# Experts' up/gate bias: from a product on TensorE to a copy by ScalarE into the PSUM bank

## The chip, the core and the metric

One core of a Trainium2 chip runs the whole program. The metric is device time in microseconds, the median over repeated runs; lower is better.

## What is computed

The reference is a transformer block on x of 2 x 2048 tokens, 256 wide, in float32: attention with a latent of 64 and 16 heads, then two rounds (C = 2) of a mixture of experts with a shared expert. What the change touches is one round's experts:

```python
h = jnp.einsum('nh,ehi->eni', xf, exp_Wup) + exp_bup[:, None, :]
h = jax.nn.silu(jnp.einsum('eni,eij->enj', h, exp_Wg) + exp_bg[:, None, :]) * h
eo = jnp.einsum('eni,eih->enh', h, exp_Wdown) + exp_bdown[:, None, :]
combined = jnp.einsum('ne,enh->nh', weights, eo)
```

Six experts, of which each token takes two. The biases are not zero in the inputs.

## The kernel before

`build` runs the attention first and then `build_mixture`, whose engine programs are in `build_tokens`. Every engine has its program written out by hand; semaphores (`S[...]`) order them. Float32 operands are split in a hi part (rounded for the matrix engine) and a lo part, and a product is three products: hi by hi, hi by lo, lo by hi.

A round goes over 8 blocks of 512 tokens: router, choice of two experts per token (`choose`), shared expert. The tokens of one batch element (a group of 4 blocks) are then scattered by GpSimd to `x_slots` in DRAM, sorted by expert in tiles of 128 rows that belong to one expert each (37 tiles a group). The expert stage `tiles(c)` of round c runs over 2 x 37 tiles: `tiles(0)` and `tiles(1)` are 148 tiles. While a group's tiles run, GpSimd scatters the second group or gathers the first one's results, and VectorE adds gathered rows (`add_first`, `add_second`, at every other tile from a group's sixth on in the second half of the stage) and normalizes a finished block (`normalize`, at three tiles of each stage).

One expert tile t goes through these steps, all in double buffers (t % 2):

- SyncE `load_tile` (L1282): slots to `xg`, four buffers; in the queue's program, load of t+3 stands ahead of the store of t-3, which waits until ScalarE has written that tile's result.
- TensorE `turn_tile` (L1599): reads the tile's expert number into a register (L1596, one load per tile), two transposes. Then `tile_up`: a product that writes the expert's up and gate bias (512 columns) into the bank `TU + t % 2`, made of a one-hot column `pick` and the table `W["bias"]` (L1604, hi and lo rows in one product), and six products of 512 columns onto it (L1615). `turn_gated` (L1628): two transposes. `tile_down`: the down bias (L1604, 256 columns) and six products of 256 columns (L1645).
- ScalarE: `tile_hi` (L1784) hi half of the tile, `tile_silu` (L1790), `tile_ghi` (L1796) hi half of the gated rows, `tile_out` (L1802) result to `eo`, `square` (L1810) for the normalization. In the loop over t they stand in the order silu(t), out(t-2), ghi(t-1), hi(t+2), square.
- VectorE: `tile_gated` (L2318), `tile_glo` (L2322), `tile_lo` (L2311), in the order gated(t), glo(t-1), lo(t+2), then adds and normalizations.

TensorE's order in the loop:

```python
for t in range(first, end + 2):
    if t < end:
        tile_up(t)
    if t == 0:
        shared_down(7)
    if t - 2 >= first:
        tile_down(t - 2)
    if first <= t - 1 < end:
        turn_gated(t - 1)
    if t + 2 < end:
        turn_tile(t + 2)
```

So the tiles t-2, t-1, t and t+2 are in flight at once. `tile_up(t)` waits for the hi and lo halves of the tile and, as its bank is that of t-2, for gated(t-2).

In `tiles(1)` SyncE also reads ahead, for the blocks to be finished, the accumulator (`load_acc`, L1301) and the layer's input x1 (L1303), 512 KB each, at four tiles, and at one tile `load_kept` (L1313, L1314), four transfers of 512 KB.

Of the kernel before, what the change touches and what calls it, by code (L numbers as in the profile page):

```python
# [21 lines left out]
F32 = mybir.dt.float32  # L22
# [1116 lines left out]
def build_tokens(nc, W, F, w, x_v, out_v, y_v, x_slots, e_slots, acc_dram, x1_dram):  # L1139

    with ExitStack() as ctx:
        names = ["small_in", "stage0", "stage1", "filled",
                 "down_in0", "down_in1", "down_in2", "down_in3",
                 "router_hi", "router_lo", "w_hi", "w_lo", "made", "bias_made", "share_bias", "own_bias", "bias_sum", "bias_hi", "bias_lo",
# [9 lines left out]
                 "t_x", "t_hi", "t_lo", "t_up", "t_silu", "t_g", "t_turned", "t_ghi", "t_glo", "t_down", "t_out",  # L1154
# [30 lines left out]
        xt_late = yy[:, :, 0:DT, :]  # L1185

# [4 lines left out]
        def x1_rows(r):  # L1191

            return x1t[:, r % 2] if r < 14 else xcur[:, 0, r % 2]
# [13 lines left out]
        def group_tiles(g):  # L1207
            return range(TILES * g, TILES * (g + 1))

# [13 lines left out]
        with nc.Block() as block:  # L1223
            @block.sync
            def _(sp):
# [45 lines left out]

                def load_tile(t):
# [16 lines left out]
                def load_acc(r):  # L1289
# [12 lines left out]
                    if r >= 8:  # L1302
                        sp.dma_start(x1t[:, r % 2], x1_dram[r - 8]).then_inc(S[f"x1_in{r % 2}"], DMA)  # L1303

                def load_x1(r):
                    sp.wait_ge(S["out_ready"], TPB * (r - 9))
# [38 lines left out]
                for r in blocks(0):  # L1345
# [62 lines left out]
            def _(pe):  # L1408
# [177 lines left out]
                def turn_tile(t):  # L1586
# [9 lines left out]
                    expert[t] = pe.value_load(F["tile_i"][0:1, g % 2, s:s + 1], min_val=0, max_val=E - 1)  # L1596
# [5 lines left out]
                def tile_bias(out, t, cols):  # L1602
                    pick = F["pick"][:, t // TILES % 2, t % TILES:t % TILES + 1].broadcast_to([P, P])
                    return pe.matmul(out, pick, W["bias"][:, cols], start=True, stop=False)  # L1604
# [26 lines left out]
                def tile_down(t):  # L1631
# [10 lines left out]
                    tile_bias(out, t, slice(2 * I, 2 * I + D))  # L1642
# [44 lines left out]
            def _(act):  # L1687
# [63 lines left out]
                def bias_hi():  # L1751
                    act.wait_ge(S["bias_sum"], 4)
                    act.wait_ge(S["filled"], FILLS)
                    act.activation(W["bias"][0:E, :], W["exp_biases"][:, :], ACT.Copy).then_inc(S["bias_hi"], 1)
# [42 lines left out]

                def tile_out(t):
# [757 lines left out]
```

## Time and profile before

| | us |
|---|---|
| median of three runs | 2874.68 |
| lowest, highest | 2870.64, 2879.78 |
| the profiled execution | 2871.32 |
| its span | 2868.5 |

Busy shares of the span: TensorE 93%, its weight loads 77%, VectorE 69%, GpSimd 67%, ScalarE 60%. The attention takes most of the time; of the experts' part, the up products (L1615) are 235.2 us for 888 instructions, the mean of one 401 ns (ends of products are modelled, so neighbours overlap). How to read it: a stage's limit is read from the engine that has no idle time in it, and the distance between the starts of neighbouring products tells what one costs, not its duration.

### The profile page before, as it was taken

The page shows a single profiled execution, that of the slowest core. Times are in us where ns is not written, and L with a number is a line of the kernel's source. Part 1 is how long each engine was busy: PE and PEld are TensorE (multiplying, and loading weights), DVE is VectorE, ACT ScalarE, POOL GpSimd, SP SyncE. Part 2 cuts the span into 40 slices and gives each one's busy share as a digit, 9 for nine tenths or more (in the row PEclk, how much of TensorE's full clock was granted, in tenths as well). Part 3 has the DMA queues.
Part 4 walks back from the last instruction along what each step waited for, and adds up shares of the span by engine and source line. Part 5 has one row for each costly group of instructions (what it writes and reads, how often), then busy time and mean ns, then how long its engine had stood idle before and what let it go on. Part 6 is the DMA issues. An engine that isn't in the chain of part 4 may idle for free. (4 is left out here: it accounts for less than half of the span.)

```text
span 2868.5 us, 47472 instructions
## 1 busy us (share of the span) xinstructions
PE 2681.7 (93%) x13656; PEld 2222.5 (77%) x13656; DVE 1975.1 (69%) x4387; ACT 1724.2 (60%) x4016; POOL 1933.7 (67%) x1735
## 2 busy tenths in 40 slices
PE   7999999999989999999999999799989998879994
PEld 5688888888777888888878888688878887768873
DVE  6688788887887788788887887255744464753455
ACT  2577777777776777777777777633323442224442
POOL 2598998998878888988988989722442232543224
PEclk8799999999999999999999999899999998879997
DMA  3011111111111010111110100154333451224552
GB/s 71 14 40 47 39 40 47 36 33 43 36 42 36 25 27 22 27 33 25 27 33 24 23 23 21 46 178 135 118 125 122 139 151 55 94 98 142 178 164 91
DMA packets 162064, 191.53 MB, mean 67 GB/s; under 512 B 57996, under 2 KB 126866, under 8 KB 161304
## 3 DMA queue, kind: packets, MB, share of 16 engines
q1 hardware_dynamic: 148504, 154.67, 18.6%
q0 software_dynamic: 12288, 33.57, 3.6%
q8 instruction: 122, 2.00, 0.3%
q14 instruction: 126, 1.03, 0.1%
q10 hardware_dynamic: 1024, 0.26, 0.0%
HBM read 114.45 MB, written 83.14 MB: 69 GB/s over the span
## 5 line engine op out<-in xcount | busy, mean ns | idle before, releaser
L305 POOL TENSOR_TENSOR pl<-pr,ph 128x512 fp32r<-128x512 f32 (+3 forms) x1184 | 1373.9, 1184 | 211.2 <-ACT ph L723 189.4
L720 ACT ACTIVATE pr<-ps 128x512 f32<-128x512 f32 (+3 forms) x1280 | 688.0, 538 | 401.6 <-PE ps L473 161.6
L995 DVE TENSOR_REDUCE part<-ps 128x1 f32<-128x512 f32 (+3 forms) x1152 | 704.0, 617 | 137.7 <-PE ps L458 122.5
L723 ACT ACTIVATE ph<-ps 128x512 fp32r<-128x512 f32 (+3 forms) x1280 | 686.7, 537 | 0.0
L458 PE MATMUL ps<-k_hi,q_parts 128*128 128x512 f32 (+3 forms) x1280 | 493.2, 386 | 41.5 <-DVE part L995 36.1
L472 PE MATMUL ps<-q_parts,k_hi 128*128 128x512 f32 (+3 forms) x1280 | 482.5, 377 | 0.3
L473 PE MATMUL ps<-q_row,k_lo 65*128 65x512 f32 (+3 forms) x1280 | 471.3, 368 | 0.0
L458 PEld LDWEIGHTS ps<-k_hi,q_parts 128*128 128x128 f32 x1280 | 243.8, 191 | 137.1 <-DVE part L995 57.9
L472 PEld LDWEIGHTS ps<-q_parts,k_hi 128*128 128x128 f32 x1280 | 242.1, 189 | 55.5 <-ACT ph L723 7.6
L473 PEld LDWEIGHTS ps<-q_row,k_lo 65*128 65x128 f32 x1280 | 242.7, 190 | 34.1
L1895 POOL DMA_INDIRECT x_slots<-xcur,slot_i x128 | 126.1, 985 | 167.7 <-PE ps L1615 80.4
L493 PE MATMUL ps<-ph,nn 128*128 128x512 f32 (+3 forms) x640 | 236.4, 369 | 1.1 <-POOL pl L305 1.1
L493 PE MATMUL ps<-ph,v_hi 128*128 128x512 f32 (+3 forms) x640 | 235.6, 368 | 1.1 <-POOL pl L305 0.9
L1615 PE MATMUL ps<-exp_up,yy 128*128 x888 | 235.2, 401 | 0.0
L494 PE MATMUL ps<-ph,nn 128*128 128x512 f32 (+3 forms) x640 | 234.3, 366 | 0.0
L495 PE MATMUL ps<-pl,nn 128*128 128x512 f32 (+3 forms) x640 | 234.1, 366 | 0.0
L494 PE MATMUL ps<-ph,v_lo 128*128 128x512 f32 (+3 forms) x640 | 233.3, 365 | 0.0
L495 PE MATMUL ps<-pl,v_hi 128*128 128x512 f32 (+3 forms) x640 | 233.3, 364 | 0.0
L904 DVE TENSOR_TENSOR ps<-ps,mask_kq 128x128 f32<-128x128 f32 x512 | 149.9, 293 | 114.2 <-PE ps L473 108.3
L1490 PE MATMUL ps<-xt,share_up 128*128 128x512 f32 x720 | 206.2, 447 | 20.1 <-issue 13.4
L815 POOL TENSOR_TENSOR q_parts<-q_raw,q_parts 64x512 fp32r<-64x512 f32 x128 | 171.2, 1338 | 51.7 <-DVE q_parts L898 41.9
L1907 POOL DMA_INDIRECT yg<-e_slots,slot_i x96 | 92.5, 964 | 163.5 <-PE ps L1615 82.2
(251 smaller groups left out, 4680.1 us busy)
## 6 DMA issues: line engine op xcount, KB each, us to landing
work<-x_slots SPq DMA_DIRECT2D x148, 128.0 KB
e_slots<-work SPq DMA_DIRECT2D x148, 128.0 KB
rec<-recip_rows SPq DMA_DIRECT2D x128, 128.0 KB
y_latent<-y_sums SPq DMA_DIRECT2D x128, 128.0 KB
yg<-y_latent SPq DMA_DIRECT2D x32, 512.0 KB
x_slots<-zero_rows SPq DMA_DIRECT2D x32, 296.0 KB
acc_shared<-accw SPq DMA_DIRECT2D x14, 512.0 KB
accr<-acc_shared SPq DMA_DIRECT2D x12, 512.0 KB, 3.7
```

The lines of the kernel that those rows point to most:

```text
L305: eng.tensor_tensor(pl[:, s % RING, 0:w], pr[:, s % PR_RING, 0:w], f32(ph[:, s % RING, 0:w]), ALU.subtract).then_inc(sem, 1)
L458: pe.matmul(ps[:, MAX_BANK + m % 2, 0:w], qa[half][:, i * P:(i + 1) * P], khs[seq][:, c * BLK:c * BLK + w], start=True, stop=True).then_in ...
L472: pe.matmul(out, khs[p // PAIRS][:, k], qa[half][:, q], start=True, stop=False)
L473: pe.matmul(out, kls[p // PAIRS][0:LD + 1, k], qc[half][:, q], start=False, stop=True).then_inc(S["scored"], 1)
L493: pe.matmul(out, v_hi[:, kt, :], ph[:, b, 0:w], start=kt == 0, stop=False)
L494: pe.matmul(out, v_lo[:, kt, :], ph[:, b, 0:w], start=False, stop=False)
L495: pe.matmul(out, v_hi[:, kt, :], pl[:, b, 0:w], start=False, stop=kt == TPB * (qb + 1) - 1).then_inc(S["latent_used"], 1)
L720: act.activation(pr[:, s % PR_RING, 0:w], src, ACT.Exp).then_inc(S["probs"], 1)
L723: act.activation(ph[:, s % RING, 0:w], src, ACT.Exp).then_inc(S["probs_hi"], 1)
L995: ins = dve.tensor_reduce(dst, src[:, 0:w], AX.X, ALU.max)
L1490: mm = pe.matmul(out, sup[:, a, kind, n, dt, m * P:(m + 1) * P], x_t[:, x, dt, :], start=i == 0, stop=i == len(terms) - 1)
L1615: mm = pe.matmul(out, tx[:, t % 2, x, dt, :], wu[:, b, bass.ds(expert[t], 1), dt, :], start=False, stop=n == len(terms) - 1)
```

## The change

- `tile_bias` is called for the down part alone, and `W["bias"]` shrinks from 768 to 256 columns. The six up products no longer start with a product that clears the bank; all of them add.
- ScalarE's new `tile_seed(t)` copies the expert's 512 bias values, the same in every partition, from a table in SBUF (`x1_table`, six experts) into the tile's bank, at an address made from the expert's number in a register. `tile_up(t)` waits for it instead of for gated(t-2); the seed waits for gated(t-2).
- The table comes from DRAM: SyncE stores the biases when they are complete (block 4) and reads them back broadcast to 128 partitions, 1.5 MB, in block 7, when layer input buffers of the first round, whose memory the table takes, are done.
- ScalarE's order in the loop becomes silu(t), ghi(t-1), hi(t+2), seed(t+2), out(t-2), square.
- The expert numbers are loaded eight at a time (five at a group's end) by TensorE and by ScalarE, without the bounds check that stood behind each load.
- x1 of the blocks 8 to 11 is read into the shared expert's buffer `gg` instead of `x1t`; so the hi part of the gated rows of block 14 waits until these blocks are out. Three small work arrays of VectorE share memory.

```diff
+        def load_experts(engine, t):
+            g, s = t // TILES, t % TILES
+            count = min(EXPERTS_AT_ONCE, TILES - s)
+            _, values = nc.values_load_multi_w_load_instructions(
+                F["tile_i"][0:1, g % 2, s:s + count], engines=[engine], min_val=0, max_val=E - 1,
+                skip_runtime_bounds_check_because="a tile's expert is a sum of five comparisons, so it is 0 to 5")
+            return {t + n: v for n, v in enumerate(values)}
...
+                def keep_biases():
+                    sp.wait_ge(S["bias_sum"], 4)
+                    sp.dma_start(bias_dram, W["exp_biases"][:, :]).then_inc(S["bias_kept"], DMA)
+
+                def load_up_table():
+                    sp.wait_ge(S["bias_kept"], DMA)
+                    sp.wait_ge(S["x_norm"], TPB * 8)
+                    for k in range(2):
+                        sp.wait_ge(S[f"x1_stored{k}"], DMA * 4)
+                    sp.dma_start(up_table, bias_dram[:, 0:2 * I].unsqueeze(0).broadcast_to([P, E, 2 * I])).then_inc(S["up_table_in"], DMA)
...
                     if r >= 8:
-                        sp.dma_start(x1t[:, r % 2], x1_dram[r - 8]).then_inc(S[f"x1_in{r % 2}"], DMA)
+                        sp.dma_start(x1g[:, r % 2], x1_dram[r - 8]).then_inc(S[f"x1_in{r % 2}"], DMA)
 
                 def load_x1(r):
-                    sp.wait_ge(S["out_ready"], TPB * (r - 9))
+                    sp.wait_ge(S["t_seed"], 4 * TILES)
...
+                    if r == 4:
+                        keep_biases()
+                    if r == 7:
+                        load_up_table()
...
-                    expert[t] = pe.value_load(F["tile_i"][0:1, g % 2, s:s + 1], min_val=0, max_val=E - 1)
+                    if s % EXPERTS_AT_ONCE == 0:
+                        expert.update(load_experts(mybir.EngineType.PE, t))
...
                 def tile_up(t):
                     pe.wait_ge(S["t_hi"], t + 1)
                     pe.wait_ge(S["t_lo"], t + 1)
-                    if t % (2 * TILES) >= 2:
-                        pe.wait_ge(S["t_g"], t - 1)
+                    pe.wait_ge(S["t_seed"], t + 1)
                     out = ps[:, TU + t % 2, :]
-                    tile_bias(out, t, slice(0, 2 * I))
...
-                                       start=False, stop=n == len(terms) - 1)
+                                       start=False, stop=n == len(terms) - 1, skip_group_check=True)
...
+                        if r == LATE[0]:
+                            act.wait_ge(S["out_ready"], 4 * TPB)
                         act.activation(gg[:, 0, m, :], g0[:, m, :], ACT.Copy).then_inc(S["g_hi"], 1)
...
+                def tile_seed(t):
+                    g, s = t // TILES, t % TILES
+                    if s == 0:
+                        act.wait_ge(S["tiles"], g + 1)
+                    if t == 0:
+                        act.wait_ge(S["up_table_in"], DMA)
+                    if s % EXPERTS_AT_ONCE == 0:
+                        seeds.update(load_experts(mybir.EngineType.Activation, t))
+                    if t % (2 * TILES) < 2:
+                        act.wait_ge(S["gated"], 4 * (LATE[0] if t >= 2 * TILES else 8))
+                    else:
+                        act.wait_ge(S["t_g"], t - 1)
+                    act.activation(ps[:, TU + t % 2, :], up_table[:, bass.ds(seeds.pop(t), 1), :].rearrange("p a n -> p (a n)"),
+                                   ACT.Copy).then_inc(S["t_seed"], 1)
...
+                    tile_seed(first)
                     tile_hi(first)
+                    tile_seed(first + 1)
                     tile_hi(first + 1)
                     for t in range(first, end + 2):
                         if t < end:
                             tile_silu(t)
-                        if t - 2 >= first:
-                            tile_out(t - 2)
                         if first <= t - 1 < end:
                             tile_ghi(t - 1)
                         if t + 2 < end:
                             tile_hi(t + 2)
+                            tile_seed(t + 2)
+                        if t - 2 >= first:
+                            tile_out(t - 2)
```

## Rows read from the trace of the kernel before

**Rows 1.** The page's first part: busy us (share of the span) and instructions per engine.

```profile
PE 2681.7 (93%) x13656; PEld 2222.5 (77%) x13656; DVE 1975.1 (69%) x4387; ACT 1724.2 (60%) x4016; POOL 1933.7 (67%) x1735
```

**Rows 2.** Busy us by stretch: length, PE, PEld, DVE, ACT, POOL, PEclk, DMA share, GB/s.

```profile
2150.00:2408.00 258.00, 246.46 (x1444) 214.24 (x1444) 124.39 (x324) 110.04 (x341) 68.47 (x70) 0.96 0.40 125
2555.00:2792.00 237.00, 225.66 (x1352) 196.04 (x1352) 119.46 (x320) 105.04 (x333) 66.22 (x69) 0.98 0.47 150
```

**Rows 3.** Timeline of one tile, TensorE: start us, us, engine line op, idle before.

```profile
2328.40 0.28 PE L1604 MATMUL ps<-bias,pick 128*128 128x256 f32 x1
...
2329.23 0.38 PE L1628 MATMUL ps<-ident,work 128*128 128x128 f32 x2
...
2329.59 0.48 PE L1604 MATMUL ps<-bias,pick 128*128 128x512 f32 x1
...
2329.91 1.56 PE L1615 MATMUL ps<-exp_up,yy 128*128 x6
...
2331.07 0.19 PEld L1604 LDWEIGHTS ps<-bias,pick 128*128 128x128 f32 x1
2331.30 0.28 PE L1604 MATMUL ps<-bias,pick 128*128 128x256 f32 x1
```

**Rows 4.** The same timeline, ScalarE, VectorE and SyncE's queue.

```profile
2328.60 0.39 ACT L1790 ACTIVATE work<-ps 128x256 f32<-128x256 f32 x1 [1.13 <-PE ps L1615]
...
2329.43 0.38 ACT L1802 ACTIVATE work<-ps 128x256 f32<-128x256 f32 x1 [0.45 <-PE ps L1645]
...
2329.72 0.38 ACT L1796 ACTIVATE nn<-ps 128x256 fp32r<-128x256 f32 x1
2329.84 0.32 SPq L1287 DMA_DIRECT2D e_slots<-work  x1
...
2329.98 0.39 ACT L1784 ACTIVATE yy<-ps 128x256 fp32r<-128x256 f32 x1
2330.13 0.42 DVE L2322 TENSOR_TENSOR nn<-ps,nn 128x256 fp32r<-128x256 f32 x1 [0.68 <-ACT nn L1796]
2330.21 0.43 SPq L1282 DMA_DIRECT2D work<-x_slots  x1
2330.47 0.41 DVE L2311 TENSOR_TENSOR yy<-ps,yy 128x256 fp32r<-128x256 f32 x1
...
2332.25 0.36 ACT L1790 ACTIVATE work<-ps 128x256 f32<-128x256 f32 x1
...
2332.64 0.43 DVE L2318 TENSOR_TENSOR work<-ps,work 128x256 f32<-128x256 f32 x1 [0.85 <-PE ps L1628]
```

**Rows 5.** Groups by line and shape, ScalarE: busy us, mean ns, idle before.

```profile
L1749 ACT ACTIVATE nn<-yg 128x512 fp32r<-128x512 f32 x6 | 3.5, 623 | 2.8 <-DMA yg<-in_exp_down 2.8
```

**Rows 6.** Line 1596, TensorE's sequencer, whole span: ns min/median/max, first and last start.

```profile
L1596 PEldq TENSOR_LOAD <-tile_i x148: 295/301/762, 2150.8 to 2777.2; - x148
L1596 PEldq FUSED_REGOPS  x148: 151/151/165, 2151.4 to 2777.5; - x148
L1596 PEldq SEQ_ASSERT  x148: 18/18/28, 2151.6 to 2777.7; - x148
```

**Rows 7.** One number load (line's view, short window), and its tile's transposes (timeline).

```profile
L1596 PEldq TENSOR_LOAD <-tile_i x1: 297/297/297, 2270.2 to 2270.2; - x1
...
2271.09 0.25 PEld L1599 LDWEIGHTS ps<-ident,work 128*128 128x128 f32 x2
```

**Rows 8.** Timeline at a tile with two scatters: ScalarE's copy-out, TensorE's weight loads.

```profile
2194.09 0.38 ACT L1802 ACTIVATE work<-ps 128x256 f32<-128x256 f32 x1 [1.32 <-PE ps L1645]
...
2195.28 0.19 PEld L1604 LDWEIGHTS ps<-bias,pick 128*128 128x128 f32 x1 [0.47 <-ACT nn L1796]
2196.65 0.20 PEld L1599 LDWEIGHTS ps<-ident,work 128*128 128x128 f32 x2 [0.18 <-issue]
```

**Rows 9.** Timeline, TensorE's weight loads at two of the six normalization tiles.

```profile
2322.27 0.19 PEld L1604 LDWEIGHTS ps<-bias,pick 128*128 128x128 f32 x1 [0.20 <-issue]
...
2724.29 0.18 PEld L1604 LDWEIGHTS ps<-bias,pick 128*128 128x128 f32 x1 [1.54 <-issue]
```

**Rows 10.** Timeline, second stretch: a late tile load and the transposes that wait for it.

```profile
2699.30 0.82 SPq L1282 DMA_DIRECT2D work<-x_slots  x1
...
2707.99 0.20 PEld L1599 LDWEIGHTS ps<-ident,work 128*128 128x128 f32 x2 [2.79 <-DMA work<-x_slots]
```

More of the change, by code:

```diff
@@ L1136, with build_tokens @@
 LATE = (14, 15)
-def build_tokens(nc, W, F, w, x_v, out_v, y_v, x_slots, e_slots, acc_dram, x1_dram):
+def build_tokens(nc, W, F, w, x_v, out_v, y_v, x_slots, e_slots, acc_dram, x1_dram, bias_dram):
     with ExitStack() as ctx:
@@ L1185, in build_tokens @@
         xt_late = yy[:, :, 0:DT, :]
+        up_table = F["x1_table"][:, :, :]
+        x1g = f32(gg[:, :, :, :]).rearrange("p a m n -> p (a m n)").rearrange("p (k j d) -> p k j d", k=2, d=D)
         def acc_rows(r):
@@ L1191, in x1_rows @@
         def x1_rows(r):
-            return x1t[:, r % 2] if r < 14 else xcur[:, 0, r % 2]
+            return x1g[:, r % 2] if r < 12 else x1t[:, r % 2] if r < 14 else xcur[:, 0, r % 2]
         T_BANK, DOWN_BANK, COUNT_BANK = 6, 4, 2
@@ L1600, in turn_tile, with tile_bias @@
                     mm.then_inc(S["t_x"], 1)
-                def tile_bias(out, t, cols):
+                def tile_bias(out, t):
                     pick = F["pick"][:, t // TILES % 2, t % TILES:t % TILES + 1].broadcast_to([P, P])
-                    return pe.matmul(out, pick, W["bias"][:, cols], start=True, stop=False)
+                    return pe.matmul(out, pick, W["bias"][:, :], start=True, stop=False)
                 def tile_up(t):
@@ L1641, in tile_down @@
                     out = ps[:, TD + t % 2, 0:D]
-                    tile_bias(out, t, slice(2 * I, 2 * I + D))
+                    tile_bias(out, t)
                     terms = [(x, b, it) for x, b in ((0, down_hi), (0, down_lo), (1, down_hi)) for it in range(2)]
@@ L1753, in bias_hi @@
                     act.wait_ge(S["filled"], FILLS)
-                    act.activation(W["bias"][0:E, :], W["exp_biases"][:, :], ACT.Copy).then_inc(S["bias_hi"], 1)
+                    act.activation(W["bias"][0:E, :], W["exp_biases"][:, 2 * I:2 * I + D], ACT.Copy).then_inc(S["bias_hi"], 1)
                 def block_of(r):
@@ L2203, in bias_lo @@
                     dve.wait_ge(S["bias_hi"], 1)
-                    dve.tensor_tensor(W["bias"][32:32 + E, :], W["exp_biases"][:, :], f32(W["bias"][0:E, :]), ALU.subtract).then_inc(S["bias_lo"], 1)
+                    dve.tensor_tensor(W["bias"][32:32 + E, :], W["exp_biases"][:, 2 * I:2 * I + D], f32(W["bias"][0:E, :]), ALU.subtract).then_inc(S["bias_lo"], 1)
                 def add_first(u):
@@ L2436, in build_tokens @@
         clear_semaphores(nc, S.values())
+EXPERTS_AT_ONCE = 8
 FILLS = 6 + TILES + 2
@@ L2458, in build_mixture @@
     x1_dram = nc.dram_tensor("x1_kept", [NBLK, P, TPB, D], F32).ap()
+    bias_dram = nc.dram_tensor("bias_kept", [E, 2 * I + D], F32).ap()
     with ExitStack() as ctx:
@@ L2466, in build_mixture @@
         W["router"] = sb("router", [P, 2, ROUNDS, DT, E], F32R)
-        W["bias"] = sb("bias", [P, 2 * I + D], F32R)
+        W["bias"] = sb("bias", [P, D], F32R)
         W["exp_up_bias"] = sb("exp_up_bias", [P, 2, E, E])
@@ L2483, in build_mixture @@
              "gate": sb("gate", [P, TPB, E]), "biased": sb("biased", [P, TPB, E]), "rank": sb("rank", [P, TPB, E]),
-             "beaten": sb("beaten", [P, TPB, E, E]), "equal": sb("equal", [P, TPB, E, E]),
+             "pairs": sb("pairs", [P, 2, TPB, E, E]),
              "diff": sb("diff", [P, TPB]), "tanh": sb("tanh", [P, TPB]),
@@ L2491, in build_mixture @@
              "picked": sb("picked", [P, JT, E]), "slot_f": sb("slot_f", [P, 2, JT]), "slot_i": sb("slot_i", [P, 2, 2, JT], I32),
-             "over": sb("over", [P, TILES, E - 1]), "tile_f": sb("tile_f", [P, TILES]), "tile_i": sb("tile_i", [P, 2, TILES], I32),
+             "tile_f": sb("tile_f", [P, TILES]), "tile_i": sb("tile_i", [P, 2, TILES], I32),
              "own_parts": sb("own_parts", [P, E])}
+        F["beaten"], F["equal"] = F["pairs"][:, 0], F["pairs"][:, 1]
+        F["over"] = F["pairs"][:, :, :, :, :].rearrange("p a j d e -> p (a j d e)")[:, 0:TILES * (E - 1)].rearrange("p (t e) -> p t e", e=E - 1)
+        F["x1t"] = F["x1_table"][:, 0:4, :].rearrange("p e (j d) -> p (e j) d", d=D).rearrange("p (r j) d -> p r j d", r=2)
         early = F["accr"][:, :, :, :].rearrange("p r j d -> p (r j d)")
@@ L2498, in build_mixture @@
         y_v = y_dram.rearrange("b q p h n -> (b q) p h n")
-        build_tokens(nc, W, F, w, x_v, out_v, y_v, x_slots, e_slots, acc_dram, x1_dram)
+        build_tokens(nc, W, F, w, x_v, out_v, y_v, x_slots, e_slots, acc_dram, x1_dram, bias_dram)
 def build(nc, w, out):
```

7 lines of the change are left out of this document (4 added, 3 removed).

## The prediction

> **What bounds the kernel now.** I read the busy shares first [rows 1]: TensorE is busy 93% of the span, nothing else above 69%. Then the table by stage [rows 2]: the change works in the two stretches in which the 148 expert tiles run, 2150 to 2408 and 2555 to 2792 us; there TensorE is busy 246.5 of 258 and 225.7 of 237 us, at a granted clock of 0.96 and 0.98 (nearly always the upper level, 2.4 GHz), while ScalarE is busy 110 and 105 us. Then one tile in order of time. On TensorE [rows 3] the down bias starts at 2328.40 and the next tile's at 2331.30: 2.90 us for a tile. Between these: the down products to 2329.23, four transposes (gated rows, then the tile after next), the up/gate bias at 2329.59, the six up/gate products from 2329.91, which take 1.39 us together, so 0.23 us for one of 512 columns. Nothing in that cycle is idle. Call the start of a tile's silu U (2328.60, when its up products are done). The other engines [rows 4]: silu at U, the copy-out of tile t-2 at U+0.83, the hi half of the gated rows at U+1.12, the hi half of tile t+2 at U+1.38; VectorE's lo halves at U+1.53 and U+1.87; SyncE's store at U+1.24 and, behind it, the load of tile t+5 at U+1.61. The stage is a stream of TensorE with all else in its shadow.
>
> **The sum, part by part.**
>
> *The up/gate bias product goes.* 148 instructions of 512 columns. The six neighbours give 1.39/6 = 0.23 each; the trace puts 0.32 between the bias's start and the next one's [rows 3], but a start there also waits for the transposes ahead. I take 0.23, since the same 2.90 also holds 7 x 0.12 for the down part and 4 x 0.11 for transposes. 148 x 0.232 = 34.3 us; 0.32 would be 47. New period 2.67 us.
>
> *The seed on ScalarE comes.* One copy of 128x512 from SBUF to PSUM per tile. The trace has none with this destination; the nearest is 128x512 from SBUF to SBUF at 0.62 us [rows 5], and a copy of half that size is 0.38 [rows 4]. So 0.4 to 0.65, I take 0.62, the same shape. Its place: after the hi half of t+2, so from about U+1.7 to U+2.3; the copy-out of t-2 then ends near U+2.6, and the next silu is due at U+2.67. The consumer, TensorE's up products of t+2, starts at U+2.67+1.31 = U+3.98. The seed has 1.7 us to spare. It waits for the gated product of tile t, done at U+0.84, long before. So its cost is zero under cover of TensorE's stream; without that cover it would be 0.6 a tile, 90 us.
>
> *Tiles with a gather-add.* In every other tile of a group's second half VectorE adds two gathered rows after its lo halves, and the square that follows pushes the next silu from its due 2331.50 to 2332.25, the gated product to 2332.64 [rows 4]. At a period of 2.67 that silu comes at U'+0.98 (U' the next tile's U), its gated product ends at U'+1.8, and the lo half of the gated rows behind it ends at U'+2.15. TensorE asks for it at U'+2.24 (its weight load for the down bias starts 0.43 ahead of the next silu's due time [rows 3]). Spare 0.1 us: it fits, barely. I book nothing, and a rival below.
>
> *VectorE's normalizations.* Six tiles have, behind the adds, four or eight more row operations, and TensorE sits idle 0.20 us (first stretch) or 1.54 (second) until VectorE is through [rows 9]. Those chains don't get shorter, so these six tiles don't gain: -1.4 us.
>
> *The scatter pauses.* In nine tiles of the groups' first halves TensorE is idle about 0.47 and 0.18 us [rows 8]. There ScalarE's copy-out starts 0.9 us late (idle 1.32 before it, against 0.45 in an ordinary tile), and the two hi halves stand behind it. In the new order the copy-out stands last, starting near U+2.3, and the late release (about U+1.75 in this row) falls before that. The nine cycles lose 0.35 to 0.6 us each, 4.5 together. What releases the copy-out isn't named by the trace, so I take two thirds: +3.0, bounds 0 and 4.5.
>
> *What the copy-out's move costs.* SyncE's queue holds store(t-2) ahead of load(t+5). With the copy-out 1.4 us later against U, the load goes out near U+3.0. Its reader is the transpose of tile t+5 at U + 3 periods + 0.74. Time for a load's data was 9.44 - 1.61 = 7.8 us, and becomes 8.75 - 3.0 = 5.7. One load was late already: issued at 2699.30 behind four transfers of 512 KB, its data let the transposes go at 2707.99, after 2.79 us of idleness [rows 10]. This one waits 2.1 us more (1.4 from the move, 0.7 from three shorter tiles): -2.1. At the four places where an accumulator and an x1 block (1 MB) are read ahead in the second stretch, no wait shows now, so data took under 7.8 us; half of the 2 MB case's 8.65 plus a little puts them near 5.5. I book -1.3 for all, bounds 0 and -6.
>
> *Expert numbers.* Now one load per tile on TensorE's sequencer, 0.30 us, with 0.15 and 0.02 of register work behind it [rows 6]; it starts at 2270.2 where the transposes' weights load at 2271.09 [rows 7], so 0.89 us of queued work covers 0.47. A load of eight, every eighth tile (20 per engine), costs between 0.30 (one instruction) and 8 x 0.30 = 2.4. I take the low end, 0.3 to 0.5, as it is one instruction for all: covered on both engines, and the bounds check goes. On ScalarE it stands before a seed with 1.7 us to spare. Nothing.
>
> *Around the stages.* The 1.5 MB table goes out on SyncE behind the down weights, some 15 us before the first seed, when that queue has nothing but one store to issue; x1's new place in the shared layer's buffer and the wait before the last shared block are met long before. First tiles: the second tile of the first stretch waits for a load anyway, -0.3 us for it and similar. The ending: the last gated rows no longer queue behind a copy-out, +0.3 twice, +0.5.
>
> Sum: 34.3 - 1.4 + 3.0 - 2.1 - 1.3 - 0.3 + 0.5 = 32.7 us. The profiled execution took 2871.3 us (span 2868.5 and 2.8 around it); the median is 3.4 above it and the three runs spread over 9. 2871.3 - 32.7 = 2838.6; from the median it would be 2842. I say 2840.
>
> **The rivals.**
>
> *A, numbers come one by one.* If eight numbers cost 8 x 0.30 = 2.4 us, TensorE is short of 2.4 - 0.89 = 1.5 us at 16 of the loads and 0.6 at the four of five numbers: 26.6 us, leaving 6: 2865. Against it: one instruction per load. If the cost per further number is part of this, anything between 2840 and 2865. Chance 0.11, middle 2855.
>
> The Trainium skill (Runtime: NRT & Kernel Launch, on instruction fetch) says that register loads cost about 200 ns per register even in bulk, from device memory. By that, as an estimate, eight would take 1.6 us, short of 0.7 at 16 loads and 0.1 at four, 12 us in all, 2851. The row of one number, 0.30 from SBUF, neither confirms nor denies it. I give it 0.08 of the 0.11.
>
> *B, the loop over ScalarE and VectorE ends last in the gather-add tiles.* For it: 0.1 us to spare by my reckoning. Price: at most the gained 0.23 in 32 tiles, 7 us: 2847. Chance 0.12.
>
> *C, no gain: TensorE's sequencer is the true bound,* its register work and dispatch hidden so far under the bias product. For it: the 0.18 idle at the transposes right after a pause [rows 8], where the queue had run dry and the number load showed. Against: products take time by columns, 0.23 and 0.12, which a dispatch limit would not give, and the number loads themselves get fewer. Then 2865 to 2875. Chance 0.05.
>
> *D, slower: tile loads become the bound.* Each load is now issued behind a later store; the loop closes if 3 periods < 2.3 us + the load's latency, so it exceeds the old 2.90 when loads take over 6.4 us. Place: the 40 tiles of the second stretch after 2670 us, where out, x1 and accumulator traffic share the queue. If all of them took the 8.65 us of [rows 10], the period there were 3.65: 40 x 0.75 = 30 us lost there, and of the gain outside only 25 remain: 2876, and up to 2890 with the first stretch's last third. Against: a single late load in 148. Chance 0.04.
>
> **How the numbers follow.** My forecast (0.68) spans 2831 to 2850 by itself: the low end with all of the pauses and no late load, the high end with none of the pauses (+3) and loads late (+5). The range 2830 to 2860 adds B and half of A, and leaves out under 0.2. This kernel's measurement can tell 0.3%, 8.6 us, from no change. Faster: 0.68 + 0.12 + most of A = 0.90. Same: C and the end of A, 0.06. Slower: D, 0.04.
>
> **What would show it.** Right: starts of the up products 2.67 us apart; no idle TensorE at tiles with two scatters; in the normalization tiles idle times longer by about 0.23; the load behind the 2 MB late by about 4.9; number loads about 0.3 to 0.5 us, 20 on each engine; the stretch between the two tile stages unchanged at about 147 us. Wrong: a number load above 0.9 us and idle time at each eighth tile (A); TensorE waiting for the gated rows' lo half in every other tile of a group's second half (B); tiles of 2.90 with idle time under "issue" (C); waits on the slot loads spread over many tiles (D). Idle TensorE behind the seed itself would break my claim that 1.7 us are to spare.

## The result, and the profile after

The changed kernel takes 2859.66 us (median of 20 runs, 2846.36 to 2875.56), the kernel before in the same series 2871.34 (20 runs). The ratio is 0.9958, 95% interval 0.9944 to 0.9972: faster by 12 us where 33 were forecast. Below, times that come from different series are compared by their ratio to the kernel before, times 2871.3 us; 0.9958 is then -12.1 us. The 2859.66 us are at the very end of the forecast's range of 2830 to 2860, and outside the 2831 to 2850 of the forecast by itself.

The profiled execution took 2857.66 us. Its busy shares, to be held against [rows 1]:

```profile
span 2855.9 us, 47200 instructions
...
PE 2654.8 (93%) x13508; PEld 2198.6 (77%) x13508; DVE 1971.6 (69%) x4387; ACT 1799.7 (63%) x4164; POOL 1935.0 (68%) x1735
```

148 products fewer on TensorE, 148 instructions and 75 us more on ScalarE. The total says little. I cut the span at four events: the transposes of a stretch's first tile, and those of the block that follows it. The table by window between these, first of the kernel before (this answers to [rows 2] with exact edges), then of the one after; the columns are those of [rows 2]:

```profile
2152.90:2384.30 231.40, 225.62 (x1356) 196.74 (x1356) 114.84 (x299) 103.49 (x328) 66.08 (x69) 0.98 0.42 131
2384.30:2557.40 173.10, 142.86 (x696) 121.60 (x697) 102.50 (x265) 40.73 (x92) 83.39 (x80) 0.81 0.24 83
2557.40:2789.20 231.80, 222.59 (x1333) 193.42 (x1333) 115.56 (x307) 103.13 (x328) 65.83 (x68) 0.98 0.48 152
```

```profile
2150.60:2374.60 224.00, 211.40 (x1283) 184.43 (x1283) 113.28 (x299) 140.65 (x401) 66.67 (x69) 0.97 0.43 135
2374.60:2547.90 173.30, 141.66 (x696) 120.67 (x696) 103.59 (x264) 41.20 (x93) 83.43 (x80) 0.82 0.24 83
2547.90:2783.20 235.30, 210.97 (x1258) 182.24 (x1258) 115.16 (x307) 141.05 (x401) 67.74 (x68) 0.97 0.46 150
```

TensorE's busy time fell by 14.2 and 11.6 us in the two expert stretches. But the first got only 7.4 us shorter, and the second 3.5 us longer. So TensorE now stands idle 6.8 and 15.1 us more. The middle is unchanged. So 3.9 of the span's 12.6 us lie in the stretches. The rest is outside: the first stretch begins 2.3 us earlier, and what follows the second is 72.7 instead of 79.3 us. Over all traces of this study the first stretch begins between 2150.4 and 2163.8, and the ending of all but this one lasts 76.2 to 81.1, so I give these 9 us to no part of the change.

An undisturbed tile, as in [rows 3]. TensorE's weight loads from one down bias to the next, and ScalarE's work of that tile:

```profile
2226.13 0.19 PEld L1631 LDWEIGHTS ps<-bias,pick 128*128 128x128 f32 x1
...
2227.51 1.24 PEld L1640 LDWEIGHTS ps<-exp_up,yy 128*128 128x128 f32 x6
2228.79 0.19 PEld L1631 LDWEIGHTS ps<-bias,pick 128*128 128x128 f32 x1
```

```profile
2226.55 0.38 ACT L1817 ACTIVATE work<-ps 128x256 f32<-128x256 f32 x1 [0.16 <-PE ps L1640]
2227.60 0.39 ACT L1823 ACTIVATE nn<-ps 128x256 fp32r<-128x256 f32 x1 [0.66 <-PE ps L1653]
2227.88 0.38 ACT L1811 ACTIVATE yy<-ps 128x256 fp32r<-128x256 f32 x1
2228.14 0.61 ACT L1839 ACTIVATE ps<-x_table 128x512 f32 x1
2228.66 0.39 ACT L1846 ACTIVATE work<-ps 128x256 f32<-128x256 f32 x1
```

The period is 2.66 us instead of 2.90, nothing in it is idle, and the seed takes 0.61 us. The core of the forecast is there. The loss sits in single tiles. TensorE's weight loads with more than a microsecond of idleness ahead of them, one of each kind:

```profile
2258.50 0.20 PEld L1626 LDWEIGHTS ps<-ident,work 128*128 128x128 f32 x2 [1.47 <-issue]
...
2696.20 0.29 PEld L1626 LDWEIGHTS ps<-ident,work 128*128 128x128 f32 x2 [3.16 <-issue]
2696.47 2.26 PEld L1640 LDWEIGHTS ps<-exp_up,yy 128*128 128x128 f32 x6
...
2743.24 0.18 PEld L1631 LDWEIGHTS ps<-bias,pick 128*128 128x128 f32 x1 [2.16 <-issue]
```

The first kind comes at each eighth tile of the groups 1 and 3: 1.2 to 1.8 us at eight tiles and 0.55 or 0.60 at the last load of a group, of five numbers. (A group is one batch element's 37 tiles; the groups 0 and 1 are the first stretch, 2 and 3 the second.) The line of the number loads says why, whole span and then a short window around the row above (minimum, median, maximum in ns):

```profile
L1216 ACTq TENSOR_LOAD <-tile_i x20: 542/1047/1772, 2147.8 to 2760.7; - x20
L1216 PEldq TENSOR_LOAD <-tile_i x20: 587/1092/2238, 2148.1 to 2758.8; - x20
```

```profile
L1216 PEldq TENSOR_LOAD <-tile_i x1: 2159/2159/2159, 2256.3 to 2256.3; - x1
L1216 ACTq TENSOR_LOAD <-tile_i x1: 1766/1766/1766, 2259.0 to 2259.0; - x1
```

In the groups 0 and 2 eight numbers take 0.59 to 0.61 us on TensorE's sequencer (0.78 for the very first load), in 1 and 3 they take 2.0 to 2.24 for the same instruction. The second kind is late tile loads, as in [rows 10], but now several: waits of 1.78, 3.16, 3.36 and 1.93 us in the second stretch, against the one of 2.79 before. The tile behind a long wait pays again. TensorE's products after the 3.16 us (timeline), and the window over them:

```profile
2696.23 0.66 PE L1626 MATMUL ps<-ident,work 128*128 128x128 f32 x2 [2.96 <-DMA work<-x_slots]
2696.54 2.81 PE L1640 MATMUL ps<-exp_up,yy 128*128 x6
...
2699.30 0.40 PE L1670 MATMUL ps<-nn 128*128 x2
```

```profile
2696.30:2697.90 1.60, 1.60 (x5) 1.38 (x6) 0.42 (x1) 0.98 (x3) 0.00 (x0) 0.50 0.62 224
```

The granted clock is 0.50, the lower level (1.2 GHz), and six up products that take about 1.6 us at the upper one take 2.81. The third kind, 1.92 to 2.16 us, is the normalization tiles of [rows 9]. Beside these three kinds one tile of the second stretch waits 1.12 us at 2673.8, while GpSimd issues gathers one behind the other; the end of the experiments comes back to it.

### The profile page after: what moved, and what is told of

Same layout as the page of the kernel before. It is cut to its first block and busy times, and to the rows that moved or that the text cites. A ratio compares the mean times of both kernels' runs of the same rounds, so it can differ in the third digit from the quotient of the medians.

```text
span 2855.9 us, 47200 instructions
## 1 busy us (share of the span) xinstructions
PE 2654.8 (93%) x13508; PEld 2198.6 (77%) x13508; DVE 1971.6 (69%) x4387; ACT 1799.7 (63%) x4164; POOL 1935.0 (68%) x1735
## 5 line engine op out<-in xcount | busy, mean ns | idle before, releaser
L1640 PE MATMUL ps<-exp_up,yy 128*128 x888 | 251.8, 420 | 0.7 <-ACT yy L1811 0.7
```

## The experiments

Two costs were open: why number loads are slow in half of the groups, and why tile loads are late. All lengths below are those of the two expert stretches, cut as above, from one trace each:

| kernel | ratio to before (95%) | us by it | first | second | both |
|---|---|---|---|---|---|
| before | 1 | | 231.4 | 231.8 | 463.2 |
| after | 0.9958 (0.9944 to 0.9972) | -12.1 | 224.0 | 235.3 | 459.3 |
| rows of 40 numbers | 0.9926 (0.9906 to 0.9947) | -21.2 | 216.1 | 232.9 | 449.0 |
| before, without up/gate bias | 0.9924 (0.9908 to 0.9940) | -21.8 | 220.8 | 226.8 | 447.6 |
| numbers one by one | 0.9928 (0.9910 to 0.9946) | -20.7 | 216.5 | 227.6 | 444.1 |
| rows of 38 | one run, 2868.2 beside 2879.5 | | 223.7 | 234.1 | 457.8 |
| 40, loads a tile earlier | 0.9887 (0.9867 to 0.9907) | -32.4 | 212.3 | 218.7 | 431.0 |
| 40, ScalarE's old order | 0.9918 (0.9900 to 0.9937) | -23.5 | 222.2 | 222.1 | 444.3 |
| 40, transfers spread | 0.9896 (0.9876 to 0.9916) | -29.9 | 217.6 | 216.4 | 434.0 |
| before, loads a tile earlier | 0.9983 (0.9970 to 0.9995) | -4.9 | 228.8 | 229.7 | 458.5 |
| 40, earlier and spread | 0.9862 (0.9838 to 0.9886) | -39.6 | 212.4 | 214.9 | 427.3 |
| after, loads a tile earlier | 0.9934 (0.9912 to 0.9956) | -19.0 | 219.7 | 224.2 | 443.9 |
| 40, other double scatters | one run, 2849.4 beside 2866.7 | | 215.4 | 227.2 | 442.6 |
| 40, four numbers a load | one run, 2845.6 beside 2862.9 | | 216.5 | 226.1 | 442.6 |

The second stretch of kernels that differ only in how they read numbers (40; one by one; four) spreads over 226.1 to 232.9, so a few microseconds there are not read as an effect of their own. Part of that spread is one wait, for the same tile load: 4.05 us with rows of 40, and 2.17 and 2.14 with one and with four numbers. Each ratio is known to about 0.2%, 4 to 7 us, and so a difference of two rows to some 7 us. The three rows of one run have no interval, and are used for what their traces show, not for their time. For most kernels the ratio and the two stretches agree within 5 us; for the kernel after they differ by 8, for rows of 40 by 7, without the bias by 6.

**Rows of 40 numbers.** The table of a tile's expert has two rows, one for each parity of the group, of 37 integers: the second begins 148 bytes on. Padded, it begins 160 bytes on.

```diff
-"tile_i": sb("tile_i", [P, 2, TILES], I32)
+"tile_i": sb("tile_i", [P, 2, 40], I32)
...
-dve.tensor_copy(F["tile_i"][:, b, :], F["tile_f"][:, :])
+dve.tensor_copy(F["tile_i"][:, b, 0:TILES], F["tile_f"][:, :])
```

> The changed kernel, but each group's row of expert numbers is padded from 37 to 40 integers, so that the second group's row starts 160 bytes behind the first's instead of 148. Nothing else moves. In the changed kernel a load of eight numbers takes TensorE's sequencer 0.59 to 0.61 us in groups 0 and 2 and 2.04 to 2.24 us in groups 1 and 3. Theory ALIGN (the row's start address decides: an odd start is loaded number by number): all 16 loads of eight take about 0.6 us, the idle times of 1.2 to 1.7 us ahead of the slot transposes at each eighth tile of the odd groups go, the two tile stages (first slot transposes to the next block's transposes: 224.0 and 235.3 us) get shorter by 8 to 9 us each, and the whole by 14 to 18. Rival TRAFFIC (the odd groups run beside the gathers and the normalizations, and that slows register loads): loads stay at 2.0 us there, and the time stays.

The number loads, whole span:

```profile
L1216 ACTq TENSOR_LOAD <-tile_i x20: 540/548/975, 2156.6 to 2756.0; - x20
L1216 PEldq TENSOR_LOAD <-tile_i x20: 587/592/826, 2156.8 to 2754.6; - x20
```

All loads are quick in all groups (0.59 to 0.61 us, 0.80 to 0.83 at three of the 20), the waits at each eighth tile are gone, and the time is 9 us less than the changed kernel's by the ratios. Where the row starts decides (ALIGN); that the groups 1 and 3 run beside other traffic does not. The gain was expected larger, 14 to 18 us: the first stretch fell by 7.9, the second by only 2.4. In it the waits on tile loads came to 11.0 us instead of 10.2, the wait at the run of gathers to 2.08 instead of 1.12, and the granted clock was 0.95 instead of 0.97. The edit quickens the loads on both engines. ScalarE's slow ones (1.74 to 1.79 us) put the seed back by 1.5 us; but the idle time stands ahead of TensorE's transposes, which wait for no seed.

**The kernel before without its up/gate bias product.** The first up product starts the bank; ScalarE has no seed and the old order.

```diff
-tile_bias(out, t, slice(0, 2 * I))
...
-start=False, stop=n == len(terms) - 1)
+start=n == 0, stop=n == len(terms) - 1)
```

> The kernel before, with the up/gate bias product left out and the first up product clearing the bank: the experts' up and gate biases are missing from the result. No seed, no table, the old orders, one number load per tile. It tells what the product itself was worth under everything else of the kernel before. My theory (TensorE's stream bounds): period 2.67 us in undisturbed tiles, each stage 13 to 17 us shorter than 231.4 and 231.8 us, the whole 28 to 34 us faster. Rival (something else takes over at once, so that the product was worth little wherever it went): the stages shorten by under 8 us each even here.

Its undisturbed period is 2.66 to 2.67 us as well, so the seed costs the stream nothing. But the stretches fall by 10.6 and 5.0 us only, where 13 to 17 each were expected: with ScalarE's old order most tiles with a gather-add take 2.73 to 3.0 us, the scatter pauses grow to 0.9 us of idleness at seven of eight tiles, and one tile load is 2.65 us late as before. Rival B is real there; that the change's new order keeps it out, the experiment on the order below bears out.

**Numbers one by one.** `EXPERTS_AT_ONCE = 1`.

> The changed kernel with one expert number per load instead of eight, on TensorE and ScalarE, without the bounds check. ALIGN and TRAFFIC both: a load of one takes 0.3 us and hides, so the waits at each eighth tile go; if the eight-number loads are what the change paid, the stages come out as in the padded kernel, 8 to 9 us shorter each. If the loads had nothing to do with it (waits on slot loads at these tiles by coincidence), the stages stay at 224 and 235 us.

```profile
L1216 PEldq TENSOR_LOAD <-tile_i x148: 296/301/522, 2160.2 to 2767.9; - x148
```

A single number takes 0.30 us, as in [rows 6], wherever it lies, and all of them are covered: same time as with rows of 40. The change's batches of eight brought nothing in the aligned groups and cost in the others.

**Rows of 38 numbers.** 152 bytes, a multiple of 8 and not of 16.

```diff
-"tile_i": sb("tile_i", [P, 2, TILES], I32)
+"tile_i": sb("tile_i", [P, 2, 38], I32)
...
```

> As the padded kernel, with rows of 38 integers (the second row starts 152 bytes on: a multiple of 8, not of 16). ALIGN with a unit of 8 bytes: 0.6 us in all groups. ALIGN with a unit of 16 or 32 bytes: odd groups stay slow, at 2.0 us or at an in-between value where pairs are loaded together (about 1.1). TRAFFIC: 2.0 us in the odd groups.

```profile
L1216 PEldq TENSOR_LOAD <-tile_i x20: 589/1113/2212, 2154.6 to 2761.1; - x20
```

Slow as before: a multiple of 8 isn't enough, and it isn't the padding as such that helped.

**Four numbers a load, rows of 40.** 160 bytes are a multiple of 32 as well as of 16, so either could be the unit. Rows of 44 integers (176 bytes) would have parted the two but found no room in SBUF. So here `EXPERTS_AT_ONCE = 4`; half of the loads start at an odd multiple of 16 bytes.

> Padded rows (40 integers), four numbers per load, 38 loads on each engine; half of them start at an odd multiple of 16 bytes. Theory COUNT (an aligned load costs a fixed part and a little per number: 0.30 for one, 0.59 for eight): 0.40 to 0.45 us for four, all alike. Rival LINE (a quick load has to start at a multiple of 32 bytes): those at odd multiples of 16 take 1.1 us (four times 0.27), the others 0.4. Time and stretches like the padded kernel with eight in either case: 1.1 us goes beyond what the queue covers by 0.2 at most.

```profile
L1216 ACTq TENSOR_LOAD <-tile_i x40: 288/308/732, 2148.4 to 2757.0; - x40
L1216 PEldq TENSOR_LOAD <-tile_i x40: 311/332/563, 2148.6 to 2755.7; - x40
```

There are 40 loads on each engine, not 38, and a multiple of 16 is enough for all. Four aligned numbers cost 0.33 us, less than either side said, and eight 0.59: close to one price per 16 bytes. The loads of five numbers at a group's end, in the runs with eight a load, say the same: with rows of 40 ScalarE takes 0.54 to 0.56 us for five as for eight, and TensorE 0.59 in the groups 1 and 3 (0.81 and 0.83 in 0 and 2). Unaligned it is about one price per number: on TensorE 2.0 to 2.24 us for eight and 1.34 to 1.48 for five, so 0.25 to 0.30 each. Eight unaligned numbers lie in three pieces of 16 bytes, and yet cost far more than three times 0.3; so the number of pieces alone doesn't set the price. That the sequencer takes 16 bytes at once where the start is aligned, and goes number by number otherwise, fits all of these; it is an inference.

**Tile loads a tile earlier, rows of 40.** SyncE's program issues the load of t+4 ahead of the store of t-3, as `xg` has four buffers.

```diff
-for t in range(first, first + 3):
+for t in range(first, first + 4):
...
-if t + 3 < first + 2 * TILES:
-    load_tile(t + 3)
+if t + 4 < first + 2 * TILES:
+    load_tile(t + 4)
```

> The padded kernel, with SyncE issuing the load of slot tile t+4 instead of t+3 ahead of the store of t-3 (four instead of three tiles before the loop). In the padded kernel the second stage is 232.8 us, with TensorE idle 11.2 us ahead of slot transposes at six tiles, and the tile behind a long wait runs its six up products in 2.9 us instead of 1.4. Theory QUEUE (the change's later copy-out made the store, and behind it the load, 1.4 us later against TensorE, and the shorter tiles took 0.7 us more of the time for a load's data): one tile more, 2.67 us, takes nearly all of these waits away; second stage 222 to 226 us, first stage 2 us shorter through its third tile, whole 8 to 12 us faster than padded. Rival BANDWIDTH (the second stage moves more bytes than its shorter time allows, whenever they are asked for): waits come back a few tiles later, second stage stays above 230.

This is 11 us less than with rows of 40 alone by the ratios, 18 by the stretches. In the first stretch the waits of the third and fourth tile go, and one wait on a tile load above half a microsecond is left (0.76) in the second stretch. I took the starts of a load and of the transposes that read it, tile by tile: in ordinary tiles they are 7.83 us apart in the kernel before, 5.84 in the one after, 8.50 here. The late ones of the kernel after had their data 5.5 to 7.1 us after issue.

**ScalarE's old order, rows of 40.** The seed stays; the copy-out stands before the hi halves again.

```diff
+if t - 2 >= first:
+    tile_out(t - 2)
 if first <= t - 1 < end:
     tile_ghi(t - 1)
 if t + 2 < end:
     tile_hi(t + 2)
     tile_seed(t + 2)
-if t - 2 >= first:
-    tile_out(t - 2)
```

> The padded kernel with ScalarE's loop in the order of before: silu, copy-out, hi of gated rows, hi of t+2, then the seed. It undoes the move alone. QUEUE: the copy-out stands 1.4 us earlier, so the stores and loads too: waits on slot loads in the second stage about half as long as in the padded kernel, stage 226 to 230 us. Against that the hi halves start 0.27 us later behind the copy-out. BANDWIDTH: no change. For the pauses at tiles with two scatters: the padded kernel has 3.2 us tiles there, whatever instruction follows the silu; they stay at 3.2 us or grow by up to 0.3.

The two stretches part: the second falls by 10.8 us (waits on tile loads 3.6 us in all, instead of 11), the first grows by 6.1 (scatter pauses of 0.9 us, gather-add tiles of 2.75 us, and 3.3 us at one run of gathers, see the end of the experiments). So the late copy-out is a reason for the late loads. In these traces the change's order is worth 6 us in the first stretch and costs 11 in the second, as long as the loads are issued where they are; against the two other kernels with quick number loads (227.6 and 226.1) it costs 4 to 5.5 there.

**Transfers spread, rows of 40.** The copies of x1 go out three or four tiles after the accumulator's, the four kept transfers one every second tile; SyncE's loads stay where they are.

```diff
...
-if c and k == 10:
-    load_kept()
+if c and k in (4, 6, 21, 29):
+    load_x1g({4: 8, 6: 9, 21: 10, 29: 11}[k])
+if c and k in (8, 10, 12, 14):
+    load_kept((k - 8) // 2)
```

> The padded kernel, second stage only: the 512 KB transfers that SyncE reads ahead no longer go out in twos and fours. x1 blocks follow their accumulator some tiles later, and the four transfers of the kept blocks go at four different tiles. Same bytes, same queue. Theory BURST (a slot load is late because 1 to 2 MB stand directly ahead of it in the queue): the waits of 1.3 to 4.1 us ahead of slot transposes shrink to under 1 us each, second stage 222 to 227 us. BANDWIDTH: stays above 230.

The second stretch is 16.5 us shorter (10 to 11 against the kernels with one and with four numbers) at the same bytes, and one wait on a tile load is left, of 1.35 us. The stretch moves 163 GB/s against 152, so the bandwidth of the stretch isn't the limit, what lies ahead in the queue is (QUEUE and BURST hold, BANDWIDTH falls). SyncE's queue of the kernel with rows of 40, around its longest wait:

```profile
2709.83 0.32 SPq L1309 DMA_DIRECT2D e_slots<-work  x1
2710.19 1.94 SPq L1341 DMA_DIRECT2D out<-accr  x4
2712.18 0.45 SPq L1304 DMA_DIRECT2D work<-x_slots  x1
2712.67 0.45 SPq L1309 DMA_DIRECT2D e_slots<-work  x1
2713.52 0.32 SPq L1323 DMA_DIRECT2D accr<-acc_shared  x1
2713.89 1.76 SPq L1325 DMA_DIRECT2D gg<-x_kept  x1
2715.69 0.48 SPq L1304 DMA_DIRECT2D work<-x_slots  x1
```

and ScalarE just before:

```profile
2706.50 0.39 ACT L1811 ACTIVATE yy<-ps 128x256 fp32r<-128x256 f32 x1
2708.90 0.60 ACT L1839 ACTIVATE ps<-x_table 128x512 f32 x1 [2.02 <-DVE work L2365]
2709.44 0.37 ACT L1846 ACTIVATE work<-ps 128x256 f32<-128x256 f32 x1
```

Read together: VectorE normalizes; the seed waits 2.02 us for its gated product; the copy-out stands behind the seed; so the store goes out at 2709.83. Between it and the tile load of 2715.69 stand the output's four stores, one more tile load and store, and 1 MB of reads, of which the second alone takes 1.76 us to issue. TensorE waited 4.05 us for that one, until 2722.36.

**The kernel before, loads a tile earlier.** The same edit without the change.

> The kernel before with the earlier slot load alone, to see what it is worth there. QUEUE: its one late load (2.8 us, and 1.5 us for the tile behind it at half clock) and the wait at the first stage's third tile (2.2 us) go: 4 to 7 us faster than before, of which none is the change's. If it is worth as much here as on top of the padded kernel, the lateness was not the change's doing.

It gives 4.9 us (interval 1.4 to 8.6): the one late load and the wait at the first stretch's third tile, both there before, are gone. On rows of 40 the same edit gave 11.2 us, by the stretches 18.0 against 4.7 here. So most of the lateness came with the change.

**The changed kernel, loads a tile earlier** (rows of 37), the other half of the two-by-two.

> The changed kernel with its rows of 37 integers, and only the load one tile earlier. It prices the slow number loads when no load is late. Theory ALIGN with QUEUE: the number loads of the odd groups still take 2.0 to 2.2 us, idle ahead of the transposes of each eighth tile there 1.2 to 1.7 us, ten such loads, so 12 to 16 us more than the padded and early one in both stretches together (212.3 and 218.7), i.e. about 445 us together, and 2856 to 2860 us in all, ratio about 0.993. Rival (an idle TensorE at each eighth tile only lets the slot loads catch up, so that the two costs overlap also here): 5 to 8 us more, about 2852.

This is 6.9 us less than the changed kernel, and 13.5 us (ratios) or 12.9 us (stretches) more than the same with rows of 40. The theory's 12 to 16 fits both; the rival's 5 to 8 is less likely, though by the ratios alone it isn't ruled out.

**Both, and spread.**

> Padded rows (40 integers), the load one tile earlier, and the transfers spread over the tiles instead of in bursts. If bursts and the late load are two ways to the same waits, their gains don't add: padded and early gave a first stretch of 212.3 us and a second of 218.7, padded and spread 217.6 and 216.4. Theory QUEUE: both stretches near 212 and 214 to 216, some 3 us less than padded and early, about 2842 us against 2875 before, a ratio near 0.988. Rival (the spread transfers take the place of a slot load somewhere else once all loads are a tile earlier): no gain over padded and early, ratio 0.989 or above. Under both the six tiles with a normalization and the nine with two scatters keep their idle times.

Both stretches are as the theory had them (212.4 and 214.9), the time is better: 2830.01 us against 2866.72, 1.4% faster than the kernel before. Its interval overlaps that of the earlier loads alone (0.9887). The second stretch, 3.8 us shorter, speaks for the spreading on top, but 2.6 us of that are at one run of gathers (see below), so the gain isn't shown.

**Other double scatters, rows of 40.** Every eighth scatter is issued with its neighbour instead of every sixth.

```diff
-if 5 + n - n // 6 == i:
+if 5 + n - n // 8 == i:
```

> Padded rows, and of the scatters every eighth one goes out together with its neighbour instead of every sixth (a scatter later for some tiles, nothing left out). Theory SCATTER (two indirect DMAs in a row on GpSimd's queue hold up whatever ScalarE does behind the silu): the long tiles of 3.2 us move from the fifth place on every fifth tile to the fifth place on every seventh tile, and there are six or seven of them instead of nine. Rival (the pause belongs to something else with that period, the gathers or the number loads): they stay at tiles 12, 17, 22, 27 and 32 of a stretch.

GpSimd and ScalarE at the first such place:

```profile
2195.60 0.96 POOL L1942 DMA_INDIRECT x_slots<-xcur,slot_i  x1 [1.70 <-PE ps L1640]
2196.87 0.96 POOL L1942 DMA_INDIRECT x_slots<-xcur,slot_i  x1 [0.30 <-issue]
2198.26 0.96 POOL L1942 DMA_INDIRECT x_slots<-xcur,slot_i  x1 [0.43 <-issue]
```

```profile
2198.02 0.39 ACT L1817 ACTIVATE work<-ps 128x256 f32<-128x256 f32 x1 [0.16 <-issue]
2199.91 0.39 ACT L1823 ACTIVATE nn<-ps 128x256 fp32r<-128x256 f32 x1 [1.51 <-PE ps L1653]
```

The long tiles moved with the scatters, to every seventh tile, and are five instead of nine (six or seven were expected). In the kernel before the late instruction behind the silu was the copy-out [rows 8], here it is the hi half of the gated rows: the pause hits whatever comes next on ScalarE. Not every run of three scatters has one: with rows of 40 nine of ten do.

**The same with gathers.** Just past the middle of the second stretch GpSimd issues gathers one behind the other: three in the kernel before, with either timing of the loads, four or five in all others. No forecast or expectation had a term for it. ScalarE, GpSimd and TensorE's weight loads there, in the kernel with rows of 40 and early loads:

```profile
2662.66 0.39 ACT L1817 ACTIVATE work<-ps 128x256 f32<-128x256 f32 x1 [0.16 <-issue]
2666.21 0.38 ACT L1823 ACTIVATE nn<-ps 128x256 fp32r<-128x256 f32 x1 [3.16 <-remote]
```

```profile
2665.48 0.96 POOL L1954 DMA_INDIRECT yg<-e_slots,slot_i  x1 [0.30 <-issue]
2667.12 0.19 PEld L1631 LDWEIGHTS ps<-bias,pick 128*128 128x128 f32 x1 [2.27 <-issue]
```

This tile and the next take 5.25 and 3.77 us instead of 2.66, 3.7 us more; in the kernel before with early loads it is 0.3 more, and with rows of 40, early loads and spread transfers 1.1. A run of four gathers in the first stretch cost 0.4 us with rows of 40 and 3.7 under ScalarE's old order. That the gathers are the cause is read from their place in time; no run moved them.

## Why the prediction was off

**Right.** *The up/gate bias product goes*: period 2.66 for the 2.67 forecast, 148 x 0.23 us. *The seed*: 0.61 us for 0.62, and TensorE doesn't wait for it in an undisturbed tile. *Tiles with a gather-add*: the 0.1 us to spare was enough; these tiles take 2.66 us too, and rival B only appears under the old order of ScalarE. *VectorE's normalizations*: they don't gain; where nothing else is late these tiles take 3.1 us in the first stretch and 4.5 in the second, as before. The idle time in them is 0.60 instead of 0.20 (with rows of 40) and 1.94 instead of 1.54, so 0.40 longer where I had 0.23. *Around the stages*: the middle 173.3 for 173.1. Rival C falls with the period. Rival D's closed loop didn't come about either, since only some tiles are late, though its mechanism did.

**Expert numbers: the step that failed first.** I took a load of eight at "the low end, 0.3 to 0.5, as it is one instruction for all", and booked nothing. The row of one number [rows 6] priced neither end. In half of the groups it was 0.59 and covered, in the other half 2.0 to 2.24, beyond the 0.89 of cover [rows 7], with 1.2 to 1.8 of idleness. That is rival A's 2.4 and 1.5, at half of its places: half of its 26.6 us is 13.3, and the two kernels with early loads that differ in nothing else are 13.5 us apart. Where tile loads were late as well it is 9 us; an idle TensorE may give these time, but the difference of the two is within the noise. The Trainium skill (Runtime: NRT & Kernel Launch, Instruction fetch mechanics) has some 200 ns per register even in bulk. The runs show 2.2/8 = 0.27 us per number unaligned, above it, and 0.59/8 = 0.07 aligned, far below. The measurement decides: for these loads from SBUF neither group follows 200 ns.

**What the copy-out's move costs: the second step that failed, in size and place.** The time left for a tile's data came out as forecast (5.84 us for 5.7; SyncE's load at 2.89 us behind the silu's start for 3.0). Booked were 2.1 us more at the load behind the 2 MB, and 1.3 us for the four places with 1 MB. In the changed kernel's trace the first waits only 0.4 us more (3.16 for 2.79, where 4.9 was forecast: its data took 7.1 us and not 8.7), and the others 1.78, 3.36 and 1.93 us, so 7.1 for the 1.3 booked. The waits together grew by 7.4 us for 3.4 booked, lower clock not counted. What issuing loads a tile earlier gives agrees with this: by the ratios 6.9 us with rows of 37 and 11.2 with rows of 40, by the stretches 15 and 18, and of these 4.9 was to be had before. Three things were missing. "They near 5.5" was an average over four places that don't look alike: behind a normalization the output's four stores and 1 MB of reads fall together, and data took 6.7 us. The copy-out stands behind a seed that itself waits for VectorE's normalization, so exactly there the load is issued late. And a wait of 3 us costs about 1.2 us more through the lower clock of the tile behind it (2.81 instead of 1.6 us).

**The scatter pauses: +3.0 became 0.** I held them for a late release of the copy-out's own input. The tiles with two scatters keep some 0.5 us each (3.1 to 3.3 instead of 2.66, before 3.4 to 3.5, two of them 3.2, instead of 2.90). They follow GpSimd's back-to-back scatters and hit the instruction behind the silu, whichever it is, so moving the copy-out couldn't win them back. How a scatter holds up ScalarE isn't shown.

**The account.** From the forecast's 32.7 the runs take 3.0 for the pauses, 9 to 13.5 for the number loads, and for the tile loads what they cost beyond the 3.4 booked. Issuing loads earlier gives 6.9 to 11.2 by the ratios; less the 4.9 that the kernel before had to gain as well, the change's own part is 2 to 6.3. The larger goes with the smaller price of the number loads, so both together are 15.4, 12.0 of it not booked. That leaves 17.7 where 12.1 was measured. The rest shows without either cost: with early loads on both sides, and rows of 40, the change is worth 27.5 us (by the ratios and by the stretches alike), where the forecast without pauses and late loads comes to 33.1. Of these 5.6 the run of gathers takes 3.4 in the traces; the others are open, and within the noise. So the 32.4 us of the kernel with both removed come near the forecast by luck: they hold 4.9 that isn't the change's, which makes up for the pauses and the gathers. Open is also why the changed kernel's trace shows 8 us less gain in the two stretches than its ratio; its short ending is in that one trace.

## What to carry to other kernels

One instruction isn't one price: here a load of several integers into registers cost 0.3 us per 16 bytes where it started at a multiple of 16 bytes, and 0.27 us per number where it didn't. So pad the rows that are read in batches, or leave single loads where they are covered. Moving a cheap step to the end of an engine's loop moves everything that hangs on it, here the store and, on the same queue, the next loads; work out the time left at the worst place of the queue (bursts, stores, a step that waits for another engine), not at the average tile. Where buffers allow, issue the loads one step earlier before shortening the loop.

## What the hardware showed that I hadn't expected

- Reading integers from SBUF into TensorE's registers: one 0.30 us; four aligned to 16 bytes 0.33; eight 0.59; eight starting 148 or 152 bytes into the table 2.0 to 2.24. On ScalarE 0.28, 0.31, 0.55, and 1.74 to 1.79.
- After 3.16 us of idleness TensorE's granted clock was 0.50 over the next 1.6 us, and six products of 512 columns took 2.81 us.
- Three indirect scatters of 0.96 us each, 0.3 to 0.4 us apart on GpSimd, go with a pause of 1.5 us on ScalarE (0.66 in an ordinary tile) in nine of ten places, 0.9 us in excess, of which TensorE sees 0.5. At one place five gathers 0.3 us apart go with one of 3.16 us, and TensorE is idle for 2.27.
